# Per-token maxima of a bit-linear stage taken from turned blocks, in a two-layer transformer kernel

## The reference, cut to what matters

```python
def act_quant(x):
    scale = 127.0 / jnp.clip(jnp.max(jnp.abs(x), axis=-1, keepdims=True), 1e-05)
    return jnp.clip(jnp.round(x * scale), -128, 127) / scale
...
    h = bit_linear(x, w1)                          # 256 -> 1024, weights -1, 0, 1
    h = depthwise_conv1d(h.transpose(0, 2, 1), conv_w, conv_b)   # 3 taps along the tokens
    h = h.transpose(0, 2, 1)
    h = jax.nn.silu(h)
    return bit_linear(h, w2)                       # 1024 -> 256
```

## Time and profile before

| | us |
|---|---|
| median of 3 executions | 641.21 |
| all three | 635.3, 641.21, 641.99 |
| the profiled execution | 635.03 |
| its span, first to last instruction | 633.3 |
| TensorE, VectorE, ScalarE, GpSimd busy | 538.1, 366.0, 361.5, 194.2 |
| mean granted TensorE clock | 0.942 |
| second attention, from ScalarE's first to the last addition | 388.9 to 573.7 |
| bit-linear stage, from the first matmul to the last addition | 574.4 to 629.6 |

### The profile page before, as it was taken

One profiled execution on the slowest core, in us unless ns is written; L12 is line 12 of the kernel. 1 busy time (PEld: TensorE's weight loads), 2 busy tenths in 40 slices (PEclk: granted clock), 3 DMA queues, 4 the chain that ended last, 5 costly groups with the idle time before them and its releaser, 6 DMA issues. The chain is left out here.

```text
span 633.3 us, 14611 instructions
## 1 busy us (share of the span) xinstructions
PE 538.1 (85%) x5264; PEld 460.8 (73%) x5264; DVE 366.0 (58%) x1114; ACT 361.5 (57%) x859; POOL 194.2 (31%) x285
## 2 busy tenths in 40 slices
PE   3899999999977249999999996688999999977565
PEld 2777778888765149999999996667878888756344
DVE  3667666757664811131223103589778877866986
ACT  2678778878764003333222333378788787865544
POOL 2032535335314251111122002621333544424071
PEclk9989999999999559999999998899999999997778
DMA  6472012110201996766755523320201110000001
GB/s 164 141 201 80 27 50 75 52 50 8 73 2 31 331 374 193 278 178 210 258 167 173 166 79 87 110 85 9 93 2 51 51 51 2 3 2 1 1 0 59
DMA packets 33529, 62.79 MB, mean 99 GB/s; under 512 B 4162, under 2 KB 24467, under 8 KB 33332
## 3 DMA queue, kind: packets, MB, share of 16 engines
q1 hardware_dynamic: 29716, 47.97, 23.5%
q0 software_dynamic: 2928, 10.75, 5.8%
q10 hardware_dynamic: 816, 3.15, 1.3%
HBM read 51.11 MB, written 10.75 MB: 98 GB/s over the span
## 5 line engine op out<-in xcount | busy, mean ns | idle before, releaser
L1576 ACT ACTIVATE ex_h_t<-ex_h,b_e 128x128 f32<-128x128 f32 x168 | 48.0, 368 | 125.7 <-PE ex_h L1760 125.7
L1166 PEld LDWEIGHTS a_ring<-ident,w_all 112*125 112x125 f32 x768 | 88.7, 188 | 23.7 <-issue 12.7
L1166 PE MATMUL a_ring<-ident,w_all 112*125 112x112 f32 x768 | 100.1, 280 | 6.4 <-ACT w_all L626 6.3
L634 ACT ACTIVATE w_all<-a_ring 125x448 f32<-125x448 f32 x128 | 62.8, 542 | 45.0 <-PE a_ring L1166 45.0
L1760 PE MATMUL ex_h<-ex_xg_t,w_s 128*128 128x128 f32 x672 | 80.2, 279 | 0.3 <-issue 0.3
L1760 PEld LDWEIGHTS ex_h<-ex_xg_t,w_s 128*128 128x128 f32 x672 | 78.5, 195 | 0.5 <-issue 0.5
L869 DVE TENSOR_REDUCE a_mx<-a_s 112x2 f32<-112x750 f32 x64 | 59.6, 931 | 30.4 <-PE a_s L1157 30.4
L1779 PE MATMUL ex_y<-w_all,ex_h_t 128*128 x336 | 75.9, 379 | 0.0
L876 DVE CUSTOM_DVE_ANT_0 w_all<-a_s,mask_sb 112x375 f32<-112x375 f32 x128 | 65.4, 544 | 16.5 <-PE a_ring L36 10.9
L626 ACT ACTIVATE w_all<-w_all,a_shift 112x375 f32<-112x375 f32 x128 | 69.7, 601 | 6.6 <-DVE a_shift L881 4.8
L1682 DVE TENSOR_TENSOR ex_y_sb<-ex_y,b_all 128x256 f32<-128x256 f32 x21 | 8.9, 425 | 104.9 <-PE ex_y L1779 104.7
(11 more groups left out here) (304 smaller groups left out, 818.0 us busy)
## 6 DMA issues: line engine op xcount, KB each, us to landing
w_s<-in_L_ffn_W SPq DMA_DIRECT2D x18, 1024.0 KB, 5.5
w_all<-in_L_ffn_W SPq DMA_DIRECT2D x8, 1024.0 KB, 11.7
ct_dram<-a_ct SPq DMA_DIRECT2D x8, 752.0 KB, 4.4
a_ct<-ct_dram POOLq DMA_DIRECT2D x8, 752.0 KB
w_s<-in_L_ffn_W ACTq DMA_DIRECT2D x3, 1024.0 KB, 10.9
w_all<-in_ctx SPq DMA_DIRECT2D x8, 375.0 KB
y_slots<-ex_y_sb SPq DMA_DIRECT2D x21, 128.0 KB, 1.7
w_ud<-in_L_ffn_w SPq DMA_DIRECT2D x2, 1024.0 KB, 9.4
```

The source lines that it names most:

```text
L634: a.activation(et[:, t % 2, kc], bank("et", t, kc)[0:KP, 0:4 * S], ACT.Copy)\
L1166: last = nc.tensor.transpose(bank("et", t, kc)[0:KP, r * S:(r + 1) * S], es[:, t % 2, r, kc * KP:(kc + 1) * KP], ident[0:S, 0:S])
L1576: last = a.activation(h_t[:, i % 2, f], hb[i % 2][:, f * 128:(f + 1) * 128], ACT.Gelu, bias=b1_e[:, i % 2, f:f + 1])
```

## The change

In the bit-linear stage, `top_of` and its tile go. TensorE turns the 112 token columns of each batch in each block of `hs` (four transposes for a block and half, after silu), and VectorE takes the largest absolute value of each row of 128 turned channels from PSUM into `peak`, which now has one place per block. Both happen two blocks behind the taps; the last two of a half stand behind its last taps. `token_scale` then reduces 8 places instead of 1 or 2. ScalarE's middle tap runs one block ahead, the diagonals of half 0 stand after the first middle tap of half 1, the copy of the spread after its first silu. GpSimd rounds four blocks (GR = 4) instead of five. TensorE turns batch 7's half after block 6 instead of 5, spreads the first scales after block 2 of half 1 instead of 4, and takes the first `down_first` groups between blocks 6 and 7 of half 1.

Besides, `begin_phase` is called with `clear=False` at the second attention: the experts' semaphores are kept and cleared together with the second attention's, at the start of the bit-linear stage.

```diff
-def begin_phase():
-
-
-    if past_sems:
+def begin_phase(clear=True):
+
+
+    if past_sems and clear:
         nc.clear_and_free_semaphores(list(past_sems))
-    past_sems.clear()
+        past_sems.clear()
     past_sems.extend(phase_sems)
...
-begin_phase()
+begin_phase(first)
 with nc.Block(no_gpsimd_drain=True) as block:
...
 hq = sb("bf_hq", [128, FC, T], BF16)
-top = sb("bf_top", [128, 2, HALF])
-peak = sb("bf_peak", [S, B, 2])
+peak = sb("bf_peak", [S, B, FC])
 spread_0 = sb("bf_spread_0", [128, HALF])
...
 hr_out = sem("bf_hr_out")
-top_out = sem("bf_top_out")
 spread_out = sem("bf_spread_out")
...
-GR = 5
+GR = 4
...
 middle(half, 0)
-middle(half, 1)
+if half:
+    diagonal(0)
 for j in range(FC):
-    if j + 2 < FC:
-        middle(half, j + 2)
-    if half == 0 and j == 5:
+    if j + 1 < FC:
+        middle(half, j + 1)
+    if half == 0 and j == 6:
         upper()
     silu(half, j)
-    if half and j == 1:
-        diagonal(0)
-    if half and j == 2:
+    if half and j == 0:
         spread_copied()
...
-def top_of(half, part, first, end):
-
-    dve.wait_ge(s_out, FC * half + end)
-    v.tensor_reduce(top[:, part], hs[:, first:end, columns(half)].rearrange("p j t -> p t j"), AX.X, ALU.max,
-                    apply_absolute_value=True).then_inc(top_out, 1)
-
-def highest(half, part):
-    dve.wait_ge(a_ps, half + part + 1)
-    v.tensor_reduce(peak[:, HB * half:HB * half + HB, part], pa[part][0:S, :].rearrange("p (b f) -> p b f", b=HB),
-                    AX.X, ALU.max).then_inc(m_out, 1)
+def highest(half, j):
+    n = FC * half + j
+    dve.wait_ge(a_ps, n + 1)
+    v.tensor_reduce(peak[:, HB * half:HB * half + HB, j], pa[n % 2][0:S, :].rearrange("p (b f) -> p b f", b=HB),
+                    AX.X, ALU.max, apply_absolute_value=True).then_inc(m_out, 1)
 def token_scale(half):
-    dve.wait_ge(m_out, 2 * half + 1)
+    dve.wait_ge(m_out, FC * half + FC)
     bs = slice(HB * half, HB * half + HB)
-    scales(1, bs, peak[:, bs, 0:half + 1], 1).then_inc(a_out, 1)
+    scales(1, bs, peak[:, bs], 1).then_inc(a_out, 1)
...
         last_scales()
+    if j >= 2:
+        highest(0, j - 2)
 lower()
-top_of(0, 0, 0, FC)
+for j in range(FC - 2, FC):
+    highest(0, j)
+token_scale(0)
 for j in range(FC):
     taps(1, j)
-    if j == 0:
-        highest(0, 0)
-        token_scale(0)
-top_of(1, 0, 0, FC - 2)
-top_of(1, 1, FC - 2, FC)
-highest(1, 0)
-highest(1, 1)
+    if j >= 2:
+        highest(1, j - 2)
+for j in range(FC - 2, FC):
+    highest(1, j)
 token_scale(1)
...
-def highest(half, part):
-    pe.wait_ge(top_out, half + part + 1)
-    if half and part == 0:
-        pe.wait_ge(m_out, 1)
-    for i in range(HB):
-        last = nc.tensor.transpose(pa[part][0:S, i * 128:(i + 1) * 128], top[:, part, i * S:(i + 1) * S], ident[:])
+def highest(half, j):
+    n = FC * half + j
+    pe.wait_ge(s_out, n + 1)
+    if n >= 2:
+        pe.wait_ge(m_out, n - 1)
+    for i, b in enumerate(batches(half)):
+        last = nc.tensor.transpose(pa[n % 2][0:S, i * 128:(i + 1) * 128], hs[:, j, b * S:(b + 1) * S],
+                                   ident[:])
     last.then_inc(a_ps, 1)
 def spread(half):
     pe.wait_ge(dg, half + 1)
     if half:
-        pe.wait_ge(m_out, 3)
+        pe.wait_ge(m_out, 2 * FC)
     nc.tensor.matmul(pr[half][:, 0:HALF], ones[0:S, :],
...
     up(0, j)
-    if j == 5:
+    if j == 6:
         turned()
+    if j >= 2:
+        highest(0, j - 2)
+for j in range(FC - 2, FC):
+    highest(0, j)
 for j in range(FC):
     up(1, j)
     if j == 2:
-        highest(0, 0)
-    if j == 4:
         spread(0)
-down_first(0)
-down_first(1)
-highest(1, 0)
-down_first(2)
-highest(1, 1)
-down_first(3)
+    if j >= 2:
+        highest(1, j - 2)
+    if j >= 6:
+        down_first(j - 6)
+for j in range(FC - 2, FC):
+    highest(1, j)
+    down_first(j - FC + 4)
 spread(1)
-for j in range(4, FC):
+for j in range(GR, FC):
     down_first(j)
```

## The result

| | before | changed |
|---|---|---|
| median us (executions) | 639.55 (4) | 631.80 (4) |
| all | 635.3, 637.88, 641.21, 641.99 | 628.47, 631.0, 632.6, 632.73 |
| profiled execution | 635.03 | 631.0 |
| first matmul to last addition of the bit-linear stage | 55.16 | 49.72 |
| second attention, from ScalarE's first instruction to that of the next stage | 185.49 | 188.52 |

The ratio is 0.990, with a 95% interval of 0.9857 to 0.9942: the changed kernel is about 1% faster. The stage that was changed is 5.4 us shorter in the profile. The second attention, in which only a wait of GpSimd was shortened, is 3.0 us longer in this execution; that has to be explained.

The account below looks back on a forecast made before the run. VectorE's queue was taken to bound the bit-linear stage. Terms -2.0 - 3.2 + 0.1 + 0.2 - 0.5 = -5.4 us took the profiled 635.03 to 629.6, and the median 641.21 to 635.8; range 627.5 to 640.5.

Parts of the forecast that it names:

- More: Rival: tail at full clock (-1.2) and the whole 0.99 us at the second attention counts; -7.0 us, chance 0.40.
- VectorE, half 0: Bit-linear stage, first half: 6.89 us of strided and turned reductions become eight turned ones, 4.88 us; -2.0 us.
- VectorE, half 1: Bit-linear stage, second half: 8.26 us of reductions and waits become 4.88 plus one hand-off; -3.2 us.
- the order on ScalarE: Middle tap one block ahead: cost 0 in half 0, exposed at the head of half 1; bounds 0 and +1.3, taken +0.1.
- tail behind the second diagonals: End of the bit-linear stage: one more spread pass at half clock; bounds -1.2 and +0.9, taken +0.2 us.
- clearing: Start of the second attention: GpSimd's first issue comes earlier without semaphore clearing; bounds 0 and -0.99, taken -0.5 us.
- The signs: Marks of being right: first diagonals about 596, VectorE over 95% busy 581 to 595, second scales 613.5, TensorE's clock 1.00.
- The price of a turned reduction: VectorE in the bit-linear stage: reducing 512 turned elements from PSUM costs 0.61 us in the queue.
- the two rates of the rows: Profile rows for VectorE's reductions: 1.77 ns per element strided against 1.34 turned; the forecast went by these.
- Waits at the head of half 1: VectorE waiting for ScalarE at the start of the second half: three waits of about 0.45 us, 1.3 us.
- TensorE's cover: Bit-linear stage: at full clock a block costs TensorE 1.4 us at most, under VectorE's 1.92; cover 0.5 us.
- the row at 388.80: Profile row: TensorE did only transposes at granted clock 0.50, then got 1.00; read as transposes keeping the clock up.

Follow-up runs that it names:

- stage_only: The changed kernel with the experts' semaphores cleared where they were before, leaving only the bit-linear part; ratio to the kernel before 0.991, median 632.76 us.
- clear_only: The kernel before with only the clearing of the experts' semaphores moved to the last stage; ratio to before 0.9981 (0.996 to 1.0002), median 637.92 us.
- double_turns: The changed kernel with every set of four transposes done twice into the same bank; bit-linear stage 50.15 us, 0.43 longer.
- four_turns: The changed kernel with every set of four transposes done four times into the same bank; bit-linear stage 60.64 us, 10.9 more.
- contiguous_top: The kernel before with its strided reductions reading the same elements contiguously, in groups of neighbours; bit-linear stage 53.11 us, 2.05 less than before.

## Why the prediction was right, point by point

The time was forecast at 635.8 with a range of 627.5 to 640.5, and came out at 631.8; the ratio was forecast at -0.85% (-5.4 of 635), and is -1.0% (-0.6 to -1.4). The direction, the mechanism and the size stand. The absolute number was 4 us too high: 1.7 of it because it was hung on a median of three, 641.21, which a fourth execution moved to 639.55, and the rest because the two medians of four lie 7.75 us apart, not 5.4, in a spread of 635 to 642. With 17 executions on one chip before's median is 638.97, on another with 22 it is 634.68. The interval reaches from the forecast into the rival *More* (over 1%); by the times alone the two can't be told apart.

| term | forecast | measured |
|---|---|---|
| VectorE, half 0 (start of taps 1 of half 1, without its wait) | -2.0 | -2.0 |
| VectorE, half 1, and the order on ScalarE (to the second diagonals, the rest) | -3.2 + 0.1 | -3.5 |
| tail behind the second diagonals | +0.2 | +0.1 |
| stage | -4.9 | -5.4 in this pair of profiles, -3.7 and -4.0 in two others of the same instructions; -5.8 (-3.5 to -8) in the times of stage_only |
| clearing | -0.5 | 0.53 in GpSimd's start, 1.5 to 2.1 at the first keys, 1.2 (-0.1 to 2.6) in the times of clear_only |

- *Luck.* That the profiles gave the forecast to half a microsecond is in part chance: the same instructions took 49.72, 51.46 and 51.19 us in three profiles, with the clock at half at different places, so the gain could have been read as 3.7. The tail's +0.1 is of this kind, as the prediction said (its clock "is chance"): the tail of the changed kernel took 9.81 to 11.96 us in the profiles of kernels that left it alone.
- *The signs.* The scales of half 1 were done 39.0 us after the first matmul, 613.5 on the scale of the kernel before (613.5 forecast); the first diagonals came 21.4 after it, 595.8 there (596). VectorE was busy for 13.71 of the 14.00 us from 582 to 596, TensorE's clock was 1.00 there, but at half until 581.6, and no reduction took over 0.75 us.
- *Half 0.* Taps 1 of half 1 started 24.65 us after the first matmul before (599.10) and 23.27 after (598.68), of which 0.61 is the wait: 24.65 - 22.66 = 2.0.
- *The price of a turned reduction* was read right, 0.61 in the queue and now 0.60. The weighing of the Trainium skill's single rate (VectorE: DVE Perf Modes, "The perf-mode tier table") against the two rates of the rows came out for the rows: read contiguously, the old form takes 1.08 ns per element, and the stride costs 64% more. The table in the Trainium skill tells memories and types apart, not layouts.
- *Waits at the head of half 1* were three of 0.45, 1.3 us in all; there are two, 0.87, and the 0.4 us between them is the difference of this row. The first taps of half 1 didn't wait: `up` ran at full clock there.
- *TensorE's cover.* 0.5 us per block was forecast; it is 0.6 to 0.7 (`double_turns` uses 0.4 of it and shows no wait within the halves). The clock was up among the transposes, as the row at 388.80 said, and against the rule of the Trainium skill named in the prediction (TensorE: Matmul & The Clock Gate, "Part 4: PE-mode transpose"); `four_turns`, with sixteen float32 transposes to four matmuls, shows it more directly, at 0.99 to 1.00 from 580.5 to 626.
- *Clearing.* The start of GpSimd was right to 0.03 us. That the load would also land faster was not in the sum. Its bound of 0.99 was too narrow: 1.9 us at the load. What speaks for a collision is that the gathers' first packets come 4.5 to 4.9 us after the stage's start in either kernel, when the load in the kernels with the earlier start has little left to move: its last packet ends at 5.2 there and at 6.8 to 7.3 with the clearing as before. But this was not tested by itself, and stays open. In the last stage GpSimd's first instruction came only 0.08 us later for the second set (0.98 against 0.90 behind ScalarE's), not 0.5, and hidden as forecast.
- *What was missing* is not a term but the noise: the second attention differs by 3 us and more from one profile to the next, and with it the clock that TensorE is granted. The 6 us between before's executions, which the prediction left unexplained, are of that size; the slower ones have the lower mean clock.

## What to carry to other kernels

Price a reduction by its layout: a strided view of the last axis cost 1.77 ns per element and the same elements in order 1.08, so in this kernel a transpose on an idle TensorE and a contiguous reduction from PSUM beat it, and can be spread over the pipeline instead of standing in one piece. When two versions are compared by one profile each, compare stage by stage from the stage's own first instruction; a stage that wasn't touched had moved by 3 us, and two profiles of the same stage differed by 1.7. And never put filling work behind an instruction that may wait: what fills a pause at one place becomes the critical path when the wait grows.

## What was not expected of the hardware

- The same pause of TensorE was followed by either clock: 2.71 us ahead of the second spread by 1.2 GHz in the changed kernel and by 2.4 in `four_turns`. With 2.7 us of needless matmuls or transposes in it, 2.4 GHz was granted in both kernels that had them there, and the stage was 0.85 us shorter.
- An issue 0.53 us earlier made a load of 752 KB be used 1.5 to 2.1 us earlier: 7.6 to 8.0 us after the stage's start without the change (three profiles), 5.9 to 6.1 with it (seven) and 6.34 in one more; with the small loads late as well 5.4, 5.4 and, where TensorE itself wasn't ready before, 5.9.
- A small instruction of VectorE, on 112 x 4 numbers, took 1.05 us once in `contiguous_top` where it took 0.17 before.
